# One value product moved whole, and a shifting ring of score banks, in an attention and mixture-of-experts kernel

## The reference

```python
K = jnp.repeat(K, REPS, axis=1)          # REPS = 4 query heads share a key head
V = jnp.repeat(V, REPS, axis=1)
scores = jnp.einsum('bhqd,bhkd->bhqk', Q, K) / jnp.sqrt(jnp.float32(D_K))
attn = jax.nn.softmax(scores, axis=-1)
out = jnp.einsum('bhqk,bhkd->bhqd', attn, V)
```

## Time and profile before

| what | value |
|---|---|
| median of three runs | 1703.83 us |
| the profiled execution's own time | 1687.52 us |
| its span | 1685.8 us |
| PE busy | 1620.1 us (96%) |
| DVE busy | 1437.2 us (85%) |
| ACT busy | 1267.1 us (75%) |
| POOL busy | 566.4 us (34%) |
| granted TensorE clock, mean | 0.99 |

### The profile page before, as it was taken

The page is one execution under the profiler, slowest core; times in us unless marked ns, Lnnn a source line. Parts: engine busy times, 40 slices in busy tenths (PEclk is TensorE's granted clock), DMA queues, the critical chain, the costliest instruction groups (busy, mean ns, idle before and its releaser), DMA issues.

```text
span 1685.8 us, 38090 instructions
## 1 busy us (share of the span) xinstructions
PE 1620.1 (96%) x13713; PEld 789.9 (47%) x13714; DVE 1437.2 (85%) x1729; ACT 1267.1 (75%) x2383; POOL 566.4 (34%) x827
## 2 busy tenths in 40 slices
PE   6999999999999999999999999999999999988994
PEld 3633444444444444444444444444444444567883
DVE  5388999999999999999999999999999992476455
ACT  3126888888888888888888888888888887405662
POOL 3121243333333333333333333333333345473221
PEclk9999999999999999999999999999999999998997
DMA  7435354423232334333423222323232014495466
GB/s 220 103 107 120 48 119 113 98 67 81 83 87 68 93 71 90 73 97 72 87 69 93 68 68 68 93 68 68 69 95 69 18 43 143 154 360 193 151 215 248
DMA packets 87862, 179.03 MB, mean 106 GB/s; under 512 B 21246, under 2 KB 25342, under 8 KB 86960
## 3 DMA queue, kind: packets, MB, share of 16 engines
q1 hardware_dynamic: 50464, 87.22, 22.1%
q0 software_dynamic: 34624, 88.25, 16.6%
q10 hardware_dynamic: 2640, 1.59, 0.4%
HBM read 91.14 MB, written 86.23 MB: 105 GB/s over the span
## 4 chain that ended last, share of the span: by engine, by line
PE 91%; DMA 3%; ACT 2%; issue 2%; DVE 2%; POOL 1%; SPq 0%; ACTq 0%; DVEq 0%; POOLq 0%
PE bank L1068 35%; PE bank L1029 25%; PE bank L1058 16%; PE bank L1237 6%; PE bank L980 5%; ACT o_acc L866 1%; PE bank L1020 1%; PE bank L1266 1%; DMA at_lo<-at_parts 1%; DMA scratch<-y_rows 1%; PE bank L1280 1%; PE bank L1039 0%; DMA xs<-slots_x 0%; PE bank L970 0%; DMA sums_rec<-sums 0%
## 5 line engine op out<-in xcount | busy, mean ns | idle before, releaser
L1378 DVE TENSOR_REDUCE max_kc<-bank 128x1 f32<-128x1024 f32 x1024 | 1243.3, 1222 | 64.5 <-PE bank L1029 48.4
L889 ACT ACTIVATE arena_p<-bank 128x512 f32<-128x512 f32 x2048 | 1109.7, 595 | 172.2 <-PE bank L1058 133.4
L1068 PE MATMUL bank<-arena_p,v_cur 128*32 128x256 f32 x8192 | 653.6, 391 | 10.6 <-ACT o_acc L866 10.6
L1029 PE MATMUL bank<-k_st,q_st 48*128 48x512 f32 x2048 | 511.8, 497 | 0.8 <-ACT qf L836 0.8
L1058 PE MATMUL bank<-q_st,k_st 50*128 50x512 f32 x2048 | 440.8, 405 | 0.8 <-ACT arena_p L889 0.8
L1029 PEld LDWEIGHTS bank<-k_st,q_st 48*128 48x128 f32 x2048 | 190.6, 183 | 427.9 <-issue 398.3
L1058 PEld LDWEIGHTS bank<-q_st,k_st 50*128 50x128 f32 x2048 | 294.9, 185 | 31.7 <-ACT arena_p L889 19.0
L1068 PEld LDWEIGHTS bank<-arena_p,v_cur 128*32 128x32 f32 x8192 | 162.9, 108 | 296.2 <-issue 154.6
L529 POOL DMA_DIRECT2D sums<-o_acc x128 | 64.8, 513 | 338.4 <-ACT o_acc L866 333.4
L532 POOL DMA_DIRECT2D sums_rec<-sums x32 | 18.2, 570 | 213.2 <-DVE sums L1408 213.2
L980 PE MATMUL bank<-xT,arena_p 128*128 128x512 f32 x160 | 83.5, 636 | 2.1 <-ACT xT L827 2.1
(11 more groups left out here) (204 smaller groups left out, 1001.1 us busy)
## 6 DMA issues: line engine op xcount, KB each, us to landing
slots_x<-pad_row POOLq DMA_DIRECT2D x27, 1295.0 KB, 5.9
q_st<-q_parts SPq DMA_DIRECT2D x192, 128.0 KB, 4.7
xs<-slots_x SPq DMA_DIRECT2D x39, 259.0 KB, 2.7
q_parts<-parts SPq DMA_DIRECT2D x16, 512.0 KB, 3.2
we_raw<-in_L_ffn_expert_w POOLq DMA_DIRECT2D x8, 1024.0 KB, 6.3
at_parts<-o_hl POOLq DMA_DIRECT2D x128, 64.0 KB, 2.3
we_his<-o_hl POOLq DMA_DIRECT2D x32, 256.0 KB, 2.4
we_hi<-we_his SPq DMA_DIRECT2D x8, 1024.0 KB, 10.1
```

The source lines that it names most:

```text
L889: act.activation(probs[:, u % PRING, :], bank[:, ring_bank(("score", u)), :], ACT.Exp, scale=SCALE).then_inc(p_ready, 1)
L1029: return pe.matmul(bank[:, 2 + 2 * (m % 2) + q, :], q_st[r:r + CROW, j % SLOTS, h, qt * P:(qt + 1) * P], k_st[r:r + CROW, key_slot(j // NC ...
L1068: mm = pe.matmul(bank[32 * h:32 * h + 32, 6, half], v_cur[:, kt, :], probs[:, (REP * kt + h) % PRING, half], start=(kt == 0 and part == 0) ...
L1378: dve.reduce_max(max_kc[:, m:m + 1], bank[:, 2 + 2 * (m % 2):4 + 2 * (m % 2), :].rearrange("p a s -> p (a s)"), AX.X).then_inc(m_done, 1)
```

## The change

- The ring loses the empty entry and has 65 entries. The turned maxima take one turn, and the bank of an entry now depends on the round: `ring_bank(i, entry)`, and `maxima_bank(j)` for the maxima. Score 46 waits for the maxima's reading (`max_read`), score 47 for exponential 44, score 48 for exponential 45; before, scores 46 and 47 waited for exponentials 44 and 45 and score 48 for the reading.
- 65 is no multiple of three, so ACT's loop body holds three rounds, and it turns ten times instead of thirty. By the built programs the body has 450 instructions instead of 153 (198 and 67 of them ACTIVATE; most of the others are register arithmetic for the waits).
- ACT reads the turned maxima once, into `negated`. POOL rounds them into `shift` itself, ahead of its difference.
- In step 1 of every round but the first, both halves of the value product run ahead of the second half's maxima and of scores 6 and 7. ACT's copy of the outputs moves one exponential forward, ahead of exponential 6.

```diff
     RING.insert(REP * (MAX_T + 1), ("maxima", 0))
-    RING.insert(REP * (MAX_T + 1) + len(SBANKS), ("none", 0))
-    assert len(RING) % len(SBANKS) == 0
+    assert (N - 2) % len(SBANKS) == 0
...
-        def ring_bank(entry):
-            return SBANKS[RING.index(entry) % len(SBANKS)]
-
-        B_MAX = ring_bank(("maxima", 0))
+        def ring_bank(i, entry):
+            return SBANKS[(len(RING) * i + RING.index(entry)) % len(SBANKS)]
+
+
+        B_MAX = SBANKS[-1]
+
+        def maxima_bank(j):
+            return ring_bank(j - 1, ("maxima", 0)) if j > 0 else B_MAX
...
             def shift_lo(j):
                 pool.wait_ge(max_read, j)
+                pool.tensor_copy(shift[:, 0, :], negated).then_inc(neg_hi, 1)
+                pool.wait_ge(neg_hi, j)
...
-            def negate_maxima(j):
-                maxima = bank[0:REP * TT, B_MAX, 0:P]
+            def negate_maxima(j, turn):
                 act.wait_ge(mT_full, j + 1)
                 act.wait_ge(shift_dma, 1 + 64 * j)
-                act.activation(shift[:, 0, :], maxima, ACT.Copy, scale=-1.0).then_inc(neg_hi, 1)
-                act.wait_ge(neg_hi, j)
-                act.activation(negated, maxima, ACT.Copy, scale=-1.0).then_inc(max_read, 1)
+                act.activation(negated, bank[0:REP * TT, maxima_bank(turn), 0:P], ACT.Copy, scale=-1.0).then_inc(max_read, 1)
...
-                    if not first and u == REP * (BEHIND - 1) + 3:
+                    if not first and u == REP * (BEHIND - 1) + 2:
                         copy_outputs(i)
...
-            round_(0, False)
-            with act.Fori(1, N - 1) as i:
-                round_(i, False)
-            round_(N - 1, True)
+            round_(0, 0, False)
+            with act.Fori(0, (N - 2) // len(SBANKS)) as m:
+                for turn in range(1, len(SBANKS) + 1):
+                    round_(m * len(SBANKS) + turn, turn, False)
+            round_(N - 1, N - 1, True)
...
-                if RING[r][0] == "none":
-                    r -= len(SBANKS)
...
                 values(0)
+
+                whole = i > 0 and kt == BEHIND - 1
+                if whole:
+                    values(1)
                 if with_max:
                     max_unit(j, m + 1)
                 score_unit(i, REP * kt + 2)
                 score_unit(i, REP * kt + 3)
-                values(1)
+                if not whole:
+                    values(1)
```

More of the change, by code:

```diff
@@ L866, in copy_outputs, with round_ @@
                 act.activation(o_acc[:, :], bank[:, 6, :], ACT.Copy).then_inc(o_ready, 1)
-            def negate_maxima(j):
-                maxima = bank[0:REP * TT, B_MAX, 0:P]
+            def negate_maxima(j, turn):
                 act.wait_ge(mT_full, j + 1)
                 act.wait_ge(shift_dma, 1 + 64 * j)
-                act.activation(shift[:, 0, :], maxima, ACT.Copy, scale=-1.0).then_inc(neg_hi, 1)
-                act.wait_ge(neg_hi, j)
-                act.activation(negated, maxima, ACT.Copy, scale=-1.0).then_inc(max_read, 1)
-            def round_(i, last):
+                act.activation(negated, bank[0:REP * TT, maxima_bank(turn), 0:P], ACT.Copy, scale=-1.0).then_inc(max_read, 1)
+            def round_(i, turn, last):
                 first = isinstance(i, int) and i == 0
@@ L880, in round_ @@
                         evacuate_projection(LAST)
-                    if not first and u == REP * (BEHIND - 1) + 3:
+                    if not first and u == REP * (BEHIND - 1) + 2:
                         copy_outputs(i)
                     if u == REP * (MAX_T + 1) and not last:
-                        negate_maxima(i + 1)
+                        negate_maxima(i + 1, turn + 1)
                     act.wait_ge(s_full, UNITS * i + u + 1)
@@ L888, in round_ @@
                         act.wait_ge(pv_done, NKT * i + u // REP + 1)
-                    act.activation(probs[:, u % PRING, :], bank[:, ring_bank(("score", u)), :],
+                    act.activation(probs[:, u % PRING, :], bank[:, ring_bank(turn, ("score", u)), :],
                                    ACT.Exp, scale=SCALE).then_inc(p_ready, 1)
-            round_(0, False)
-            with act.Fori(1, N - 1) as i:
-                round_(i, False)
-            round_(N - 1, True)
+            round_(0, 0, False)
[3 more added lines that the diff above has]
+            round_(N - 1, N - 1, True)
             copy_outputs(N)
@@ L1038, in max_transpose @@
                 pe.wait_ge(maxq_ready, j + 1)
-                pe.transpose(bank[0:REP * TT, B_MAX, 0:P], max_q[:, :], ident[:, :]).then_inc(mT_full, 1)
+                pe.transpose(bank[0:REP * TT, maxima_bank(j), 0:P], max_q[:, :], ident[:, :]).then_inc(mT_full, 1)
             def ring_bank_free(i, entry):
                 r = RING.index(entry) - len(SBANKS)
-                if RING[r][0] == "none":
-                    r -= len(SBANKS)
                 kind, u = RING[r]
@@ L1057, in score_unit @@
                 r = HALVES[h % 2]
-                pe.matmul(bank[:, ring_bank(("score", u)), :], k_st[r:r + ROWS, key_slot(i // NC), kt * P:(kt + 1) * P],
+                pe.matmul(bank[:, ring_bank(i, ("score", u)), :], k_st[r:r + ROWS, key_slot(i // NC), kt * P:(kt + 1) * P],
                           q_st[r:r + ROWS, i % SLOTS, h, :], start=True, stop=True).then_inc(s_full, 1)
```

## The result

The changed kernel is slower: 1751.7 us in the median (1733 to 1782) against 1703.5, a ratio of 1.024 with a 95% interval of 1.021 to 1.027. The forecast was 1711.1 with a range of 1692 to 1720; the sign was right, the time far outside. The wide spread of the changed kernel's times belongs to the answer; it comes back with TensorE's clock.

What follows compares the result with a forecast made beforehand. TensorE was taken to bound the kernel, VectorE following. Terms -9.5 - 1.2 + 18.0 = +7.3 us on the profiled 1687.5 gave 1694.8; the median's extra 16.3 carried over made 1711.1 us, range 1692 to 1720.

Steps and rivals of the forecast that it cites:

- The copy's wait: Steps 1 and 2: the wait on the output copy goes, one on exponential 6 replaces it; 1.2 us gained in 30 rounds.
- step 11: Attention, second half of step 11: maxima take one turn of the ring, 0.305 us a round, 9.5 us gained.
- The jump: ScalarE's loop of three rounds: each of nine jumps back waits for a code packet, 18 us lost; likeliest case, 50%.
- a fetch in a crowd: At the round's end SyncE issues six query loads, so a packet's price was taken as 2.8 us.
- falls on TensorE in full: Score 3 waits for exponential 0, so the 2.0 us left of each jump's wait is lost on TensorE.
- from above 9 x 3.1 = 28: Upper bound of the loss at ScalarE's nine jumps back: 28 us.
- 1: ScalarE's loop code stays: nothing lost at the jumps, 9.5 + 1.2 gained, 1693.1 us; 27%.
- 3: Code stays and no wait follows the copy's in step 2: 21.5 us gained, 1682 us; 3%.
- Rival 2: ScalarE's jump misses cheaply: 9 x 1.1 = 9.9 us lost, 1703 us, no change; 17%.
- Rival 4: Step 11 gains 0 and ScalarE's jump misses: 1721 us; 3%.

Runs made afterwards that it cites:

- the loop of two: The kernel before with ScalarE's loop of thirty single rounds made fifteen laps of two rounds: 1803.1 us; with 68 idle instructions ahead of it, 1706.5 us.
- the loop over four pieces: The changed kernel with 40 idle instructions early in ScalarE's program, its 450-instruction loop over four pieces instead of five: 1762.9 us, 1.025.
- the nine delays of 0.58: The changed kernel written out, with one exponential too many ahead of the first one of rounds 4, 7, ... 28: 1692.7 us, 0.992.

## Why the prediction missed

**The gains were there.** Step 1 of round 15 in the kernel after, TensorE and then ScalarE; what was predicted from 757.15 on in the earlier trace rows is here counted from 761.24.

```profile
761.24 1.07 PE L1071 MATMUL bank<-arena_p,v_cur 128*32 128x256 f32 x16
762.24 0.50 PE L1034 MATMUL bank<-k_st,q_st 48*128 48x512 f32 x2
762.58 0.40 PE L1061 MATMUL bank<-q_st,k_st 50*128 50x512 f32 x2
...
763.66 0.49 PE L1061 MATMUL bank<-q_st,k_st 50*128 50x512 f32 x1 [0.21 <-ACT arena_p L893]
764.08 0.64 PE L1071 MATMUL bank<-arena_p,v_cur 128*32 128x256 f32 x8
```

```profile
762.38 0.60 ACT L872 ACTIVATE o_acc<-bank 128x512 f32<-128x512 f32 x1
763.01 2.06 ACT L893 ACTIVATE arena_p<-bank 128x512 f32<-128x512 f32 x4
```

Shifted by 4.09 us the prediction reads: products done 762.25, scores 762.59, exponential 6 at 763.03, the late score near 763.68, value product 764.11. The copy's wait gave place to exponential 6's, and 0.05 us a round came of it, against the kernel before as it was; against that kernel with the loop of three rounds nothing did (4.05 us for the stretch, above). In step 11 (TensorE, round 15) the second half is 1.24 us (787.42 to 788.66) instead of the 1.55 of the earlier trace rows:

```profile
787.42 0.50 PE L1034 MATMUL bank<-k_st,q_st 48*128 48x512 f32 x2
787.76 0.40 PE L1061 MATMUL bank<-q_st,k_st 50*128 50x512 f32 x2
788.09 0.64 PE L1071 MATMUL bank<-arena_p,v_cur 128*32 128x256 f32 x8
788.66 0.50 PE L1034 MATMUL bank<-k_st,q_st 48*128 48x512 f32 x2
```

Together 10.7 us were forecast and 10.3 found, less the 2.9 of the second turn, which the prediction didn't have. Of that cause the runs show only that it goes with the code's place. GpSimd's rounding cost nothing that shows.

**The jump was there, and at its price.** Five pieces don't stay, nine jumps miss, 17.5 us on ScalarE where 18.0 were forecast. Both terms of the price came out: the jump takes 2.7 us more than one that stays (2.92 less 0.22) where 2.8 was taken, and some 0.75 of it is hidden where 0.8 was. But the 2.8 was the middle of two transfers' times, 1.7 and 3.9, and the packet has landed 1.7 us behind the jump; the other 1.2 us, from the landing to the next instruction, stood in no term, so that the size came out is in part luck. The reason given, a fetch in a crowd, is only partly right too: without the crowd ScalarE's wait is still 1.5. And the packets were 63 instead of the 40 to 50 forecast, six for each turn of the loop.

**The step that failed** is that what is left of the wait "falls on TensorE in full", with "9 x 2.0 = 18 us lost" and "from above 9 x 3.1 = 28". It took a wait of TensorE to cost what it lasts; the lower clock behind such a wait stood at nothing in the sum. Of the 57 us that the nine rounds lost, 39.5 came after the waits, at the lower clock. The upper end of the range was worked out from the length of a fetch alone and so could not hold it, and the number of falls, which differs from run to run, makes the spread of 1733 to 1782 us (mean granted clock 0.971 to 0.939; 0.96 at 1752). The page of the kernel before had a sign of it: its clock row is full in the attention, where TensorE hardly waits, and not at the end, where it does (from 1480 to 1540 us it is busy for 51.7 of 60 us, at a granted 0.91). The page's clock row, and that stretch:

```profile
PEclk9999999999999999999999999999999999998997
```

```profile
1480.00:1540.00 60.00, 51.74 (x242) 40.65 (x241) 43.02 (x143) 16.37 (x35) 33.83 (x37) 0.91 0.86 303
```

The Trainium skill, "TensorE: Matmul & The Clock Gate", section "HAM oscillation — how this bites in real kernels", says that a TensorE which waits between pieces of work can be throttled again and start the next piece at the lower clock. The runs here agree (0.52 granted behind a wait of 1.8 us). Its example waits some 3 to 5 us for data in each piece; here single waits of 1.0 to 2.2 us in a full stream were enough, and once 0.79, and the same wait does it only sometimes. The prediction had asked the Trainium skill about the code and not about the clock.

On the code, the Trainium skill, "Runtime: NRT & Kernel Launch", section "Instruction fetch mechanics", says that a store holds 512 instructions in two blocks of 16 KiB and that a jump back out of it waits. The second agrees with the runs here. The first is no measure by itself: 303 and 450 instructions are fewer than 512, and here 303 missed at one place and stayed at another, and 450 missed at both places tried.

**The rivals.** 1 and 3 wanted the code to stay; it didn't. Rival 2 wanted a jump at 1.1 us, and there is none even in the middle of a round (the cheapest anywhere, one in the loop of two, is 1.4). Rival 4 wanted no gain in step 11, which came in full. The slowest of them, 1721 us, was still 30 short: none had the clock in it.

**What stays open.** Why one wait is followed by the lower clock and the next like it is not; it isn't the wait's length alone (in the changed kernel TensorE stood for 1.28 us in round 22 and its clock fell, for 1.66 us in round 4 and it did not). And why three pieces stay and four don't: a store of four pieces with one place taken by the next in order fits all loops here, but no run tells it from another arrangement.

## What to carry to other kernels

Before a loop's body grows, count over how many 8 KB pieces of code it lies, not only its instructions: here three stayed and four missed, and the place alone decided 97 us. A wait put on the engine that bounds the kernel is priced twice, once for its length and once for the clock behind it, and the second can be the larger. Where code is streamed in order without a wait, writing a loop out is an alternative to moving it: here it took the jump away and made each wait a constant, and was worth more (13 us) than the change itself, which, written out, the times don't tell from nothing (1691.0 us before, 1687.7 and 1689.2 after) and the rounds put at some 0.15 us each.

## What was not expected of the hardware

- An 8 KB piece of code missed at a jump back cost ScalarE 1.5 us in a quiet stretch and 1.7 to 2.3 at the round's end in the changed kernel, 1.4 to 2.7 in the loop of two; streaming in order, written out, cost nothing that shows.
- After waits of TensorE of 0.95 us and more its granted clock was at the lower level behind 33 of 58: for some 3 us of full work at the least, 34 in the changed kernel and 58 in the loop over four pieces at the most. It was so behind one of sixteen waits of 0.79 us, and never behind the nine delays of 0.58.
- An exponential that waits for two semaphores begins 0.12 us behind its score where the values are in registers, and 0.04 where they are constants. Writing the loop out, which brings this, took 0.35 us from a round of the kernel before; step 2's 0.08 of it came with longer loops in registers too.
